# Expert rows sent through memory by indirect scatters, in place of a gather by matmuls

## The reference

```
logits = x_flat @ gate_w.T                      # 512 tokens, 8 experts
scores = softmax(logits); top 2 of 8 per token; w = scores * in_topk
g, u = x @ experts_gate_up                      # 2 x 704 columns per expert
h = silu(g) * u
out = sum over the two experts of w * (h @ experts_down)
out = out + sigmoid(x @ shared_expert_gate_w.T) * shared_mlp(x)    # 1408 wide
```

## Time and profile before

| | us |
|---|---|
| median of 3 executions | 763.45 |
| lowest to highest | 762.96 to 764.26 |
| the profiled execution, its time | 764.33 |
| its span, first to last instruction | 762.3 |

### The profile page before, as it was taken

How to read it: one execution, slowest core, us unless ns; L and a number is a source line. 1 busy time by engine, 2 the same in 40 slices (tenths; PEclk the granted TensorE clock), 3 DMA queues, 4 the chain that set the end, 5 groups by cost and what they waited for, 6 DMA issues and landing times.

```text
span 762.3 us, 10295 instructions
## 1 busy us (share of the span) xinstructions
PE 742.9 (97%) x3424; PEld 609.0 (80%) x3424; DVE 592.0 (78%) x745; ACT 346.0 (45%) x472; POOL 139.5 (18%) x106
## 2 busy tenths in 40 slices
PE   7999999999999999999999998999999999999997
PEld 6888887888877888888888886788887888888875
DVE  6488886888989988999947355893648888888873
ACT  4322221222346555666624246333337666666661
POOL 4244444444400000000000022454500000000000
PEclk9999999999999999999999999999999999999999
DMA  8046557555512354232023061210235666767621
GB/s 291 0 164 193 193 193 276 193 193 172 188 56 90 117 240 175 95 100 93 28 102 161 0 255 56 83 42 1 86 122 228 227 241 245 261 233 283 264 83 56
DMA packets 28840, 115.83 MB, mean 152 GB/s; under 512 B 3664, under 2 KB 3664, under 8 KB 25744
## 3 DMA queue, kind: packets, MB, share of 16 engines
q1 hardware_dynamic: 27808, 114.19, 42.0%
q10 hardware_dynamic: 1008, 1.32, 0.5%
HBM read 114.45 MB, written 1.05 MB: 152 GB/s over the span
## 4 chain that ended last, share of the span: by engine, by line
PE 89%; DVE 7%; DMA 1%; ACT 1%; issue 1%; SPq 0%; DVEq 0%
PE ps L795 20%; PE ps L762 7%; PE ps L758 7%; PE ps L759 7%; PE ps L977 6%; PE ps L705 5%; PE ps L707 5%; PE ps L706 5%; PE ps L950 4%; PE ps L959 4%; PE ps L961 3%; PE ps L960 3%; PE ps L1006 3%; PE ps L991 2%; DMA ring<-stream 1%; PE ps L967 1%
## 5 line engine op out<-in xcount | busy, mean ns | idle before, releaser
L371 POOL TENSOR_TENSOR c_lo<-ring,c_hi 128x512 fp32r<-128x512 f32 x64 | 82.9, 1297 | 108.0 <-ACT c_hi L436 108.0
L758 PE MATMUL ps<-qk_hi,c_hi 128*128 128x512 f32 x256 | 100.3, 392 | 1.9 <-ACT c_hi L436 1.9
L1160 DVE TENSOR_TENSOR runmax<-runmax,att 128x512 f32<-128x512 f32 x64 | 98.4, 1537 | 4.3
L759 PE MATMUL ps<-qk_lo,c_hi 128*128 128x512 f32 x256 | 99.7, 389 | 0.0
L436 ACT ACTIVATE c_hi<-ring 128x512 fp32r<-128x512 f32 x64 | 40.4, 633 | 130.3 <-PE ps L762 112.9
L376 POOL TENSOR_TENSOR w_lo<-raw,w_hi 128x1024 fp32r<-128x1024 f32 x11 | 27.3, 2485 | 290.5 <-ACT w_hi L562 290.5
L1465 DVE TENSOR_TENSOR wu_lo<-raw_u,wu_hi 128x2048 fp32r<-128x2048 f32 (+1 forms) x33 | 69.5, 2106 | 7.1 <-ACT wu_hi L572 7.1
L762 PE MATMUL ps<-qk_hi,c_lo 128*128 128x512 f32 x256 | 68.5, 389 | 0.0
L795 PE MATMUL ps<-p_hi,d_hi 128*128 128x512 f32 x256 | 64.2, 393 | 0.6 <-DVE ps L1237 0.6
L1154 DVE SCALAR_TENSOR_TENSOR att<-ring,beta,ps 128x512 f32 (+1 forms) x64 | 47.8, 747 | 20.3 <-PE ps L762 19.6
L795 PE MATMUL ps<-p_hi,d_lo 128*128 128x512 f32 x256 | 63.2, 389 | 0.0
(11 more groups left out here) (287 smaller groups left out, 1555.7 us busy)
## 6 DMA issues: line engine op xcount, KB each, us to landing
ring<-stream SPq DMA_DIRECT2D x64, 512.0 KB, 4.2
raw_u<-up_in SPq DMA_DIRECT2D x22, 1024.0 KB, 5.7
ring<-ctx_in SPq DMA_DIRECT2D x32, 512.0 KB, 3.3
raw_d<-down_in SPq DMA_DIRECT2D x22, 512.0 KB, 4.8
raw<-shared_in SPq DMA_DIRECT2D x11, 768.0 KB, 4.6
raw_u<-up_last_in SPq DMA_DIRECT2D x11, 768.0 KB, 5.9
late<-wqkv_in SPq DMA_DIRECT2D x1, 3072.0 KB, 10.6
raw_d<-down_last_in SPq DMA_DIRECT2D x11, 256.0 KB, 2.7
```

The lines of the kernel that those rows point to most:

```text
L371: pool.tensor_tensor(c_lo[:, s % 2, :], ring1[:, s, 0, :], c_hi[:, s % 2, :].bitcast(F32), ALU.subtract).then_inc(lo1_ready, 1)
L758: pe.matmul(ps[:, s, :], hi, qk_hi[:, k, :], start=(k == 0), stop=False)
L759: pe.matmul(ps[:, s, :], hi, qk_lo[:, k, :], start=False, stop=False)
L1160: dve.tensor_tensor(runmax[:, :], runmax[:, :], att[:, g * U + s, :], ALU.max).then_inc(max_done, 1)
```

## The change

- A buffer `slots` in DRAM of 15 x 128 rows, 514 values each (512 of the normalised token row, the token's number, its weight).
- SP clears it during the second pass, by 15 DMAs from a zero tile `blank`, behind the late weights and ahead of the refills of `ring2` from pair 16 on.
- The normalised rows are written by ACT into `rows_n`, 514 wide. DVE works out two row numbers and two weights per token (`slot_rows`, after shared step 2). POOL sends the rows to their slots by four indirect DMAs for the tokens' first experts after its low parts of shared step 5, and by four for the second ones after step 8; DVE puts the second weight in place between (`second_weight`, after step 6, behind the first four DMAs).
- SP loads the 128 rows of each unit (263 KB) into `xgn`, between the up and the down loads. `pick`, `slot_info`, `gather`, the copy of the gathered rows on ACT, `t_hi`, `t_lo`, `places` and `unit_tables` go.
- `turn_gathered` moves ahead of the first down product; in the written orders of ACT and DVE the split of the gathered rows moves ahead of the last up chunk.
- The half tile: the 64 last down rows are loaded twice, stacked in the partitions; the high part stays in the upper half of `wd_hi` and the low part is put in the lower half, so that one matmul of 128 rows makes hi*hi and hi*lo together: five matmuls in place of six. For this the last hidden chunk is 256 wide, its last 64 columns being a repetition (one more small product on DVE). One load of 512 KB takes the place of 256 KB and 128 KB; one ACT copy takes the place of two.

```diff
+        slots = nc.dram_tensor("slots", (NU * P, ROW), F32, kind="Internal").ap()
...
             sp.dma_start(late[:, 3 * KC:LATE, :], wv_in).then_inc(wv_loaded, 16)
+            sp.wait_ge(blank_ready, 1)
+            for u in range(NU):
+                sp.dma_start(slots[u * P:(u + 1) * P, :].rearrange("p (h c) -> p h c", h=2),
+                             blank[:, :].unsqueeze(1).to_broadcast([P, 2, ROW // 2])).then_inc(cleared, 16)
             refill2(4, CT // 2 // R2)
...
+            def load_rows(u, first=False):
+                if not first:
+                    sp.wait_ge(turned_psum, u)
+                    sp.wait_ge(info_read, u)
+                sp.dma_start(xgn[:, :], slots[bass.ds(u * P, P), :]).then_inc(xg_full, 16)
...
+                if not first:
+                    load_rows(u)
                 for c in range(CH):
                     if not first:
-                        sp.wait_ge(dn_lo_ready, u * CH + (c + 1 - CH))
...
+                        if c < 2:
+                            sp.wait_ge(dn_lo_ready, u * 2 + (c + 1 - 2))
+                        else:
+                            sp.wait_ge(dn_last_ready, u)
+                    sp.dma_start(raw_d[c][:, :, :], down_in[expert_ * CH + c]).then_inc(dn_full[c], 16)
...
+            def scatter_rows(c):
+                pool.wait_ge(rows_ready, c + 1)
+                for st in range(ST):
+                    pool.indirect_dma_start(slots, bass.IndirectOffsetOnAxis(row_of[:, c, st:st + 1], 0),
+                                            rows_n[:, st, :], None).then_inc(rows_out[c], 16)
             for n in range(1, SH):
                 low_parts(n, n % RAW, n % HL)
+                if n == 5:
+                    pool.wait_ge(cleared, 16 * NU)
+                    scatter_rows(0)
+                if n == 8:
+                    scatter_rows(1)
...
                 hidden_high(u, 1)
                 if not last:
+                    gathered_high(u + 1)
                     up_high(u + 1, 2)
-                    gathered(u + 1)
-                    gathered_high(u + 1)
...
+                for t in range(2 if c < 2 else 1):
...
+                if c == 2:
+                    pe.matmul(ps[:, 2, :], hh_e[:, 2, P:2 * P], wd_hi[2][:, 1, :], start=False, stop=False)
+                    mm = pe.matmul(ps[:, 2, :], hl_e[0:HALF, 2, P:2 * P], wd_hi[2][0:HALF, 1, :], start=False, stop=True)
...
                 up(u, 2)
                 pe.wait_ge(hl_ready, u * CH + 1)
-                if not last:
-                    slot_info(u + 1)
                 turn_hidden(u, 1)
                 if not last:
-                    gather(u + 1)
-                if not first:
-                    pe.wait_ge(y_lo_ready, u)
+                    turn_gathered(u + 1)
                 down(u, 0)
-                if not last:
-                    turn_gathered(u + 1)
-                    pe.wait_ge(info_read, u + 2)
                 pe.wait_ge(hl_ready, u * CH + 2)
                 turn_hidden(u, 2)
...
                     pe.wait_ge(prod_done, SH - 1 + CREDIT)
-                    pe.wait_ge(t_lo_ready, 1)
-                    pe.wait_ge(info_ready, 1)
-                    slot_info(0)
-                    gather(0)
-                if n == SH - 1:
                     turn_gathered(0)
...
+            def slot_rows():
+                in_unit = counts[:, 0:ST * E].rearrange("p (t e) -> p t e", e=E)
+                dve.tensor_scalar(first_row[:, :], slot_row[:, 0:E], float(P), None, ALU.mult)
...
+                step(dve.tensor_tensor(row_by[:, :, :], row_by[:, :, :], in_extra[:, :, :], ALU.add))
+                for c in range(2):
+                    dve.scalar_tensor_tensor(out=carried[:, c, :, :], in0=rank[:, :, :], scalar=float(c),
+                                             in1=wn[:, :, :], op0=ALU.is_equal, op1=ALU.mult)
...
+                step(dve.tensor_copy(row_of[:, :, :], row32[:, :, :]))
+                dve.tensor_copy(rows_n[:, :, TOK], token_col[:, :])
+                dve.tensor_copy(rows_n[:, :, WGT], weight_of[:, 0, :]).then_inc(rows_ready, 1)
+            def second_weight():
+                dve.wait_ge(rows_out[0], 16 * ST)
+                dve.tensor_copy(rows_n[:, :, WGT], weight_of[:, 1, :]).then_inc(rows_ready, 1)
+            def down_last_low(u):
+                dve.wait_ge(dn_hi_ready, u * CH + CH)
+                dve.tensor_tensor(wd_lo[2][:, 0, :], raw_d[2][:, 0, :], wd_hi[2][:, 0, :].bitcast(F32), ALU.subtract)
+                dve.tensor_tensor(wd_hi[2][HALF:P, 1, :], raw_d[2][HALF:P, 1, :],
+                                  wd_hi[2][HALF:P, 1, :].bitcast(F32), ALU.subtract).then_inc(dn_last_ready, 1)
...
             def read_info(u, first=False):
+                dve.wait_ge(xg_full, u * 16 + 16)
                 if not first:
                     dve.wait_ge(back_ready, u)
+                    dve.wait_ge(prod_e_done, u * CH)
-                dve.tensor_copy(info_s[:, :], ps[:, 3, 2 * P:2 * P + 4]).then_inc(info_read, 1)
+                dve.tensor_copy(info_s[:, :], xgn[:, TOK:ROW]).then_inc(info_read, 1)
...
             def product_e(u, c):
...
+                h, g_, u_ = hid_e[:, c, 0:w], gated_e[:, c, 0:w], ps[:, c % 2, w:2 * w]
+                ins = dve.scalar_tensor_tensor(out=h, in0=g_, scalar=info_s[:, 1:2], in1=u_, op0=ALU.mult, op1=ALU.mult)
+                if w < 2 * P:
+                    ins = dve.scalar_tensor_tensor(out=hid_e[:, c, w:2 * P], in0=g_[:, P:w], scalar=info_s[:, 1:2],
+                                                   in1=u_[:, P:w], op0=ALU.mult, op1=ALU.mult)
...
                 hidden_low(u, 1)
                 if not last:
                     read_info(u + 1)
+                    gathered_low(u + 1)
                     up_low(u + 1, 2)
-                    picks(u + 2, u + 2)
-                    gathered_low(u + 1)
                 hidden_low(u, 2)
```

More of the change, by code:

```diff
@@ L28 @@
 RAW = 6
-FAR = 1024.0
+ROW = D + 2
+TOK, WGT = D, D + 1
 EPS = 1e-5
@@ L592, in output_high @@
                 act.activation(y_hi[:, :], ps[:, 2, :], ACT.Copy).then_inc(y_hi_ready, 1)
-            def gathered(u):
-                act.wait_ge(gather_psum, u + 1)
-                act.activation(xgn[:, :], ps[:, 1, :], ACT.Copy).then_inc(xgn_ready, 1)
             def gathered_high(u):
@@ L666, in _ @@
                     up_high(0, 2)
-            gathered(0)
             gathered_high(0)
@@ L971, in down @@
                 pe.wait_ge(hl_ready, u * CH + (c + 1))
-                pe.wait_ge(dn_lo_ready, u * CH + (c + 1))
-                for t in range(2):
-                    rows_ = HALF if c == 2 and t == 1 else P
-                    hi, lo = (h[0:rows_, c, t * P:(t + 1) * P] for h in (hh_e, hl_e))
+                if c < 2:
+                    pe.wait_ge(dn_lo_ready, u * 2 + (c + 1))
+                else:
+                    pe.wait_ge(dn_last_ready, u + 1)
+                for t in range(2 if c < 2 else 1):
+                    hi, lo = (h[:, c, t * P:(t + 1) * P] for h in (hh_e, hl_e))
                     for i, (a, b) in enumerate(((hi, wd_hi), (hi, wd_lo), (lo, wd_hi))):
-                        mm = pe.matmul(ps[:, 2, :], a, b[c][0:rows_, t, :], start=(c == 0 and t == 0 and i == 0),
-                                       stop=(c == 2 and t == 1 and i == 2))
+                        mm = pe.matmul(ps[:, 2, :], a, b[c][:, t, :], start=(c == 0 and t == 0 and i == 0), stop=False)
+                if c == 2:
+                    pe.matmul(ps[:, 2, :], hh_e[:, 2, P:2 * P], wd_hi[2][:, 1, :], start=False, stop=False)
+                    mm = pe.matmul(ps[:, 2, :], hl_e[0:HALF, 2, P:2 * P], wd_hi[2][0:HALF, 1, :], start=False, stop=True)
                 mm.then_inc(y_psum_e, 1)
-            def slot_info(u):
-                pe.wait_ge(pick_ready, u + 1)
-                for st in range(ST):
-                    pe.matmul(ps[:, 3, 2 * P:2 * P + 4], pick[:, st, :],
-                              info[:, st, bass.ds(u, 1), :].rearrange("p a c -> p (a c)"),
-                              start=(st == 0), stop=(st == ST - 1))
-            def gather(u):
-                for st in range(ST):
-                    for part in (t_hi, t_lo):
-                        mm = pe.matmul(ps[:, 1, :], pick[:, st, :], part[:, st, :], start=(st == 0 and part is t_hi),
-                                       stop=(st == ST - 1 and part is t_lo))
-                mm.then_inc(gather_psum, 1)
             def turn_gathered(u):
-                pe.wait_ge(xgn_ready, u + 1)
+                pe.wait_ge(xg_full, u * 16 + 16)
                 for k in range(KC):
@@ L1019, in unit @@
                 up(u, 1)
-                if first:
-                    pe.wait_ge(info_read, 1)
                 turn_hidden(u, 0)
@@ L1430, in extra_units @@
                 step(dve.tensor_copy(which[:, :], which32[:, :]))
                 dve.sem_inc(more_ready, 1)
-            def places():
-                for b in range(CH):
```

(7 more changed lines are left out.)

134 lines of the change are left out of this document (53 added, 81 removed).

## The result

The changed kernel took 759.89 us, median of 8 runs (758.38 to 761.65), beside 764.03 us for the kernel before (8 runs, 762.96 to 766.92): a ratio of 0.9931 [0.9919, 0.9943]. It is faster by 0.7%. I had forecast 744.0 us with a range of 738 to 752, so the direction was right, the size was about a fifth of what I had named, and the time lies outside my range. The profiled execution took 758.38 us with a span of 756.6, against 764.33 and 762.3.

The account below looks back on a forecast made before the run. PE was taken as the bound, busy 97% of the span, with a loop over ACT and DVE deciding after the change. Savings 2.29 + 1.13 + 15.5 + 0.46 = 19.4 us gave 744.9 profiled, 744.0 median, range 738 to 752.

Parts of the forecast that it names:

- The clearing: Second pass of the cross attention, ahead of pair 16's load: 10.6 us by bytes against 13.2 of slack, so no cost.
- rival 2: Second pass: clearing runs by packets or somewhat worse, pair 16 up to 6 us late, 745 to 750 us; chance 0.15.
- the far end: Clearing in the second pass priced by packets, 78 ns each: 18.8 us, with PE losing 5.6.
- The units: Units 1 to 9: each falls from 17.47 to 15.75 us, 1.72 saved in each, 15.5 us in all.
- The loop: Dependences over ACT and DVE, up 0's end to turn hidden 2: 11.25 us, plus 4.50 of PE, set a 15.75 us unit.
- The stacked half tile: In each unit: saves PE one matmul, 0.23 us, and adds a 64-column product, some 0.18, to the loop.
- rival 5: Units: loads come too late at 300 GB/s and the change brings less, some 748 to 752 us; chance 0.05.
- Unit 0: From its silu to unit 1's first matmul: 12.76 us become 11.63, 1.13 saved.
- The indirect DMAs: On POOL in the shared steps: four may hold it 9.1 us before PE waits; cost taken as nothing.
- Rival 3: Shared steps: indirect DMAs hold POOL, 18.3 us for four, 9.2 over, twice: 762.4 us, half likelier, 753; chance 0.12.
- rival 4: Second pass: clearing's pieces off round addresses cost far more than stores' packets; 778.8 us at 200 ns each; chance 0.05.
- the last units: End of the unit loop: the last unit follows PE and saves two matmuls, 0.46 us.

Follow-up runs that it names:

- experiment 1: Changed kernel with all 15 clearing DMAs issued behind the last refill of ring2 instead of ahead of pair 16's load: 748.31 us, ratio 0.979 to the kernel before.
- experiment 2: Changed kernel with 8 of the 15 clearing DMAs left ahead of pair 16's load and 7 behind the last refill: 750.22 us, ratio 0.9813 to the kernel before.
- experiment 3: Kernel before with only the zero tile and the 15 clearing DMAs added at the changed kernel's place, buffer unused: 778.4 us, ratio 1.018.
- experiment 5: Changed kernel, used clearing behind the last refill, 15 DMAs of 512-byte pieces to an unread buffer at the early place: 749.42 us, ratio 0.9794 to the kernel before.
- late clearing: Changed kernel with all 15 clearing DMAs moved behind the second pass's last refill of ring2: 748.31 us, ratio 0.979 to the kernel before.
- experiment 4: Changed kernel with 8 clearing DMAs early, 7 late, then 10 more stores to unread buffers in pieces of 1280 and 512 bytes: 747.91 us, single run.
- experiment 6: Changed kernel with the clearing behind the last refill, one piece of 2056 bytes per row from a wider zero tile: 745.74 us, single run.

## Why the prediction failed, step by step

**The clearing (the step that failed).** Shown by experiments 1, 2, 3 and 5. The profiled change brought 5.7 us of the 19.4; of the 13.7 missing, this step is 10.7. The slack that I read, 13.2 us, was right: it measures 13.0. The price was wrong. I had taken 10.6 us by bytes, at a cost of nothing, and 18.8 us by packets as the far end; the landing moved by 21.4. That is rival 2's mechanism, past its end, and the forecast took the cheaper of two ends with a choice ("no row shows a piece of 1 KB at the price of one of 2 KB") that only said that I didn't know. What I had left out is that a piece of 1028 bytes can cost more than a packet of 2 KB, 86 ns for 78, which makes 20.7 us of the engines' time; the remaining 0.7 are not taken apart. The far end was wrong in the same direction, as nothing was allowed above the nearest row.

**What the wait costs beyond itself.** 21.7 - 13.0 = 8.7 us is the wait; the loss was 10.67. The other 2 us are the half clock after it, which no step of mine had.

**The units.** The loop was right: its steps are 8.54 us from y_lo to turn hidden 2 and 2.90 before, 11.44 where I had 11.25, and 4.39 for 4.50. The stacked half tile makes the difference: 0.41 in the loop for the 0.18 that I had priced. In the late clearing's kernel the eight periods from the first y_lo (584.16) to the ninth (711.54) take 127.4 us, for 139.7 before (586.86 to 726.60): 12.4 saved, 13.8 forecast. Of the 1.4 missing, 0.8 are 0.1 a unit and 0.6 one unit of 16.33, in which an up load came late (rival 5's mechanism, once), and y_hi stands behind its high part on ACT:
```profile
709.11 1.92 ACT L612 ACTIVATE wu_hi<-raw_u 128x2048 fp32r<-128x2048 f32 x1 [0.37 <-DMA raw_u<-up_in]
```
The next period and the last one gave 2.1 for the 2.2 expected.

**Unit 0.** From the shared low part to the first y_lo the late clearing saves 3.35 us, for 2.29 + 1.13 forecast: right. In the changed kernel it is 1.83, because here a wait of 2.61 us at turn hidden 2 was followed by a lower clock:
```profile
586.79 0.44 PE L991 MATMUL ps<-ident,hid_e 128*128 128x128 f32 x2 [2.61 <-DVE hl_e L1500]
```
```profile
588.00:592.00 4.00, 4.00 (x12) 3.16 (x11) 3.67 (x4) 1.65 (x2) 0.00 (x0) 0.57 1.00 416
```
The late clearing has the same wait, 2.60 us, at the same place, and the clock stays at 1.00 behind it. Six profiles have this wait: the clock fell behind it in those of the changed kernel and of experiments 2 and 4, and stayed in those of experiments 1, 5 and 6. What decides is open; it is worth 1.6 us.

**The indirect DMAs.** Taken at nothing, and so it was. POOL in order of time at step 6:
```profile
518.54 1.12 POOL L417 DMA_INDIRECT slots<-rows_n,row_of  x1 [0.17 <-issue]
519.97 1.36 POOL L417 DMA_INDIRECT slots<-rows_n,row_of  x1 [0.30 <-issue]
521.63 0.96 POOL L417 DMA_INDIRECT slots<-rows_n,row_of  x1 [0.30 <-issue]
522.90 0.96 POOL L417 DMA_INDIRECT slots<-rows_n,row_of  x1 [0.30 <-issue]
523.88 2.40 POOL L398 TENSOR_TENSOR w_lo<-raw,w_hi 128x1024 fp32r<-128x1024 f32 x1
```
Four hold POOL 5.3 us, for a slack of 9.1, and PE never waits for w_lo. Rival 3 priced each at 4.57 us; the longest of all eight took 1.90, so it fell, and with it the port between DVE and POOL as a cause. The Trainium skill (DMA: Bandwidth & Descriptors, section "Anatomy of one DMA — SWDGE (gpsimd) path") gives the time of a whole DMA on this path, and by its figures the estimate was 2.6 us for one and 10.4 for four, one after the other. In the trace one landed 3.2 us after its issue (the median of eight), but POOL was held for 5.3 us by four, half the estimate, and the trace decides.

**The sum.** In the late clearing, 16.1 us of the 19.4 came (span 746.2 for 762.3). The 3.3 missing: 0.65 in the time of the shared low part, all of it there before the late weights are issued (276.87 for 276.18; the changed kernel itself had 275.91), so ahead of what the forecast was about; 1.4 in the units, 0.1 at unit 0 and 0.1 at the last units; and 1.05 behind the last y_lo (7.89 us to the end, for 6.84), where all but the first of the last eight matmuls ran at half clock, 0.43 us from start to start in place of 0.23:
```profile
740.00:742.00 2.00, 2.00 (x6) 1.54 (x5) 1.54 (x3) 0.00 (x0) 0.00 (x0) 0.50 0.14 55
```
Without the clearing's loss the changed kernel would have stood at 748 to 749, inside the range. The chances were off in one place: rival 2 and rival 4 were one unknown, the price of a piece, and together deserved more than 0.20.

## What to carry to other kernels

A transfer that nothing waits for isn't free when it stands in an ordered queue: price it against the slack of the next load behind it, by pieces as well as by bytes, and if the price of its kind of piece isn't in the trace put it behind the loads that have a due time. Before work is taken off the bounding engine, find the loop of dependences behind it and move what need not stand in it (here one low part of 2.2 us); an edit that takes work off that engine and adds to the loop, as the stacked half tile, pays only once the loop is no longer the bound.

## What the runs showed of the hardware

- Time of one DMA packet in the engines, stores from on-chip memory to memory, as means: 26 ns at 512 bytes, 69 at 1280 (distance 2560), 81 to 92 at 1028 (starts off round addresses; 86 in the changed kernel), at most 122 at 2056.
- SP's time for the 15 clearing DMAs: 21.4 us behind the weights' loads, one issue of 5.5 us among them, and then one per 1.3 to 1.5 us, the time that the engines took for the pieces of one; 11.4 us behind the last loads of the pass, 10.0 with one piece per row.
- Three DVE instructions, 128 x 512, 64 x 512, and one on all 128 again: 0.69 and 0.72 us from start to start with the middle one on the upper 64 partitions and written over its input, 0.60 and 0.61 with it on the lower 64 and written elsewhere.
- An indirect DMA of 128 rows of 2056 bytes held POOL 0.96 to 1.90 us, with 0.3 before the next, and landed in 3.2 us at the median.
- PE's clock: after 8.7 us without a matmul it was at 0.50 for the first 4.2 us of work, after 10.8 us for the first 6.0. A wait of 2.6 us was followed by 0.50 in three profiles and by 1.00 in three others. Waits of 0.8 us in every unit left it at 1.00.
